# GpSimd waits for the normalised input ahead of its clears and splits, in a four-stage transformer kernel

## The reference

```
x = x + attention0(ln(x));  x = x + mixture0(ln(x))     # 12 heads of 16, relative positions; 8 experts, relu
x = x + attention1(ln(x));  x = x + mixture1(ln(x))     # the same, tanh gelu
x = x + attention2(ln(x))                               # relative positions
t = ln(x); t = t + attention3(ln(t))                    # causal
x = x + t + mixture2(ln(t))                             # capacity-limited routing, gelu
x = x + mixture3(ln(x))                                 # 8 experts and a shared one, gelu
x = x + mixture4(ln(x))                                 # 8 experts and a shared one, gated silu

ln(v)  = (v - mean(v)) / sqrt(var(v) + eps)
expert = act(v @ W1[e] + b1[e]) @ W2[e] + b2[e]         # 192 -> 768 -> 192, weighted by a top-2 gate
```

## Time and profile before

| | value |
|---|---|
| median of three runs | 514.72 us (511.82 to 517.03) |
| the profiled execution | 511.37 us, span 509.5 us, mean granted clock 0.98 |
| TensorE matmuls busy | 463.6 us, 91% of the span |
| VectorE, ScalarE, GpSimd busy | 354.0, 234.8, 171.3 us |
| chain that ended last, by engine | PE 69%, DVE 11%, issue 10%, POOL 4%, DMA 3% |
| in it by line | L951 24%, L963 10%, L975 7%, L766 6%, L1047 3%, L391 1% |
| DMA | 62.36 MB, mean 122 GB/s |

### The profile page before, as it was taken

One profiled execution on the slowest core, in us unless ns is written; L12 is line 12 of the kernel. 1 busy time (PEld: TensorE's weight loads), 2 busy tenths in 40 slices (PEclk: granted clock), 3 DMA queues, 4 the chain that ended last, 5 costly groups with the idle time before them and its releaser, 6 DMA issues.

```text
span 509.5 us, 8914 instructions
## 1 busy us (share of the span) xinstructions
PE 463.6 (91%) x3064; PEld 382.4 (75%) x3064; DVE 354.0 (69%) x780; ACT 234.8 (46%) x594; POOL 171.3 (34%) x171
## 2 busy tenths in 40 slices
PE   4989699999889799999889988899969999989997
PEld 3755499999555499999645654555759999979997
DVE  6575588998476578998476467451179899868764
ACT  1267245544156366555156337423218555627443
POOL 6026324673025415754006214310033665500000
PEclk8999999999999989999999999999989999989999
DMA  5380025650191015551169500602313555525551
GB/s 146 121 248 1 1 96 183 184 187 1 65 305 40 0 64 196 180 175 39 43 170 322 176 0 1 186 2 93 124 37 134 185 185 176 191 58 166 200 177 36
DMA packets 19347, 62.36 MB, mean 122 GB/s; under 512 B 4025, under 2 KB 6898, under 8 KB 19314
## 3 DMA queue, kind: packets, MB, share of 16 engines
q1 hardware_dynamic: 19314, 61.93, 38.0%
HBM read 59.82 MB, written 2.10 MB: 122 GB/s over the span
## 4 chain that ended last, share of the span: by engine, by line
PE 69%; DVE 11%; issue 10%; POOL 4%; DMA 3%; ACT 1%; SPq 1%; POOLq 0%; DVEq 0%
PE bank L951 24%; PE bank L963 10%; PE bank L975 7%; PE bank L766 6%; PE bank L805 3%; PE bank L977 3%; PE bank L792 3%; DVE xn L1047 3%; PE bank L661 2%; POOL rstd L391 1%; DMA rel<-rel_scratch 1%; PE bank L653 1%; PE bank L773 1%; DVE nmax L1153 1%; PE bank L674 1%
## 5 line engine op out<-in xcount | busy, mean ns | idle before, releaser
L951 PE MATMUL bank<-xT_hi,w_hi 128*128 128x256 f32 x408 | 111.7, 295 | 0.0
L600 ACT ACTIVATE hid<-bank,b 128x256 f32<-128x256 f32 x150 | 62.7, 471 | 71.0 <-PE bank L951 70.8
L1193 DVE TENSOR_TENSOR w_lo<-w,w_hi 128x512 fp32r<-128x512 f32 x102 | 93.0, 950 | 2.2 <-ACT w_hi L552 0.3
L951 PE MATMUL bank<-xT_hi,w_lo 128*128 128x256 f32 x408 | 82.6, 284 | 0.0
L443 POOL TENSOR_TENSOR w_hl<-w,consts 128x384 fp32r<-128x384 f32 x50 | 52.4, 1048 | 85.1 <-PE bank L977 85.1
L951 PEld LDWEIGHTS bank<-xT_hi,w_hi 128*128 128x128 f32 x408 | 79.2, 194 | 1.5 <-issue 1.1
L423 POOL TENSOR_TENSOR probs<-probs,rinv 128x512 f32<-128x512 f32 (+1 forms) x44 | 42.8, 991 | 101.0 <-DVE rinv L1157 100.9
L951 PEld LDWEIGHTS bank<-xT_hi,w_lo 128*128 128x128 f32 x408 | 64.3, 194 | 0.0
L975 PE MATMUL bank<-w_hl,hid_hi 128*128 128x384 f32 x200 | 61.7, 373 | 0.0
L445 POOL TENSOR_TENSOR w_hl<-w,w_hl 128x384 fp32r<-128x384 f32 x50 | 57.9, 1158 | 3.9
L963 PE MATMUL bank<-w,hid 128*128 128x192 f32 x308 | 56.5, 327 | 2.3 <-issue 2.3
(11 more groups left out here) (159 smaller groups left out, 674.3 us busy)
## 6 DMA issues: line engine op xcount, KB each, us to landing
w<-in_M_w_dram SPq DMA_DIRECT2D x34, 768.0 KB, 5.5
w<-in_M_w_dram SPq DMA_DIRECT2D x33, 576.0 KB, 3.9
w<-in_M_w_dram SPq DMA_DIRECT2D x9, 288.0 KB, 2.9
wqkv<-in_A_wqkv_dram SPq DMA_DIRECT2D x4, 432.0 KB, 7.0
rel_scratch<-relall SPq DMA_DIRECT2D x4, 372.0 KB, 2.3
wproj<-in_A_wproj_dram SPq DMA_DIRECT2D x4, 288.0 KB, 7.9
wqkv<-in_M_w_dram SPq DMA_DIRECT2D x2, 576.0 KB, 17.4
kT<-in_M_w_dram SPq DMA_DIRECT2D x2, 576.0 KB, 6.6
```

The costliest lines, as they stand in the source:

```text
L600: ins = act.activation(hid[:, 2 * b + c, :], bank[B_H[b]][:, c * T:(c + 1) * T], FUNC[cfg["act"]], bias=b1[:, kb, bass.ds(at, 1)])
L951: ins = pe.matmul(bank[B_H[b]][:, c2 * T:(c2 + 1) * T], w, xs, start=(q == 0), stop=(q == 4))
L1193: dve.tensor_tensor(w1_cols(w1_lo, b), w1_cols(w1[s], b), w1_cols(w1_hi, b).bitcast(F32), ALU.subtract)\
```

## The change

Three lines move or are added, all on GpSimd. The clear of `q_st` goes ahead of the first power. Behind that power GpSimd waits until both tiles of the first input are normalised, and only then clears the rest. And in the front of each of the five mixtures it waits, behind the power, until both tiles of that mixture's input are normalised, before it begins to split. `nln` counts the layer norms so far, two tiles each. The waits inside the loops of the experts are as before.

```diff
@@ -391,9 +391,10 @@
                 pool.tensor_tensor(rstd[:, :], var_eps[:, :], minus_half[:, :], ALU.pow).then_inc(rstd_ready, 1)
 
             pool.memset(minus_half[:, :], -0.5).then_inc(minus_half_ready, 1)
+            pool.memset(q_st[:, :, :, :], 0.0).then_inc(pool_ready, 1)
             pool.wait_ge(minus_half_ready, 1)
             ln(0)
-            pool.memset(q_st[:, :, :, :], 0.0).then_inc(pool_ready, 1)
+            pool.wait_ge(xn_ready, TT)
             pool.memset(k_st[:, :, :, :], 0.0).then_inc(pool_ready, 1)
             pool.memset(v_st[:, :, :, :], 0.0).then_inc(pool_ready, 1)
             pool.memset(kT[:, :, :, :], 0.0).then_inc(pool_ready, 1)
@@ -457,6 +458,7 @@
                 else:
                     ln(nln)
                     nln += 1
+                    pool.wait_ge(xn_ready, TT * nln)
                     if MOE[n]["split2"]:
                         for i in range(2):
                             split(n, 0, i)
```

## The result

The changed kernel takes 498.62 us (median of four runs, 496.72 to 500.07) against 513.27 (511.79 to 517.03) for the kernel before; the ratio is 0.9718, 95% interval 0.9674 to 0.9762. The forecast was 501.0 in a range of 496.5 to 507. The profiled execution took 498.38, 13.0 less than the profiled one of before; the sum had said 13.5.

The account below looks back on a forecast made before the run. TensorE's matmuls held most of the span; the removable waits were VectorE instructions held by GpSimd. 2.75 + 10.7 = 13.5 us off the profiled 511.37 gave 497.9, with 3.35 to the median 501.2, given as 501; range 496.5 to 507.

Parts of the forecast that it names:

- the sum: Whole kernel: 2.75 us at the start plus 10.7 at the mixtures, 13.5 us less.
- (a): At the start: clear of q_st ahead of the first power, 1.38 us from about 0.85 to 2.2, costs nothing.
- (b): At the start: GpSimd waits for both normalised tiles; position products at 12.05 instead of 16.48, 2.75 us after clock loss.
- an open bound: At the start: gain only 2.0 us if the clears also hold the copy of the transposed input out of PSUM.
- (c): Waits ahead of the splits of mixtures 0, 1 and 3: 8.2 us plus 2.5 from the clock, 10.7 in sum.
- The yardstick: Mixture 4, same stages without splits: 7.22 us from power to second up-matmul block, against 10.05 in mixture 0.
- The slack for the low parts: Low parts of w1 for blocks 1 and 2: each can lose one split (0.9 us), covered by 0.4 us.
- (d): Waits at mixtures 2 and 4: no split follows, so nothing gained.
- the second case: Mixture fronts: clock still falls ahead of the first up matmuls; (c) is 8.2, sum 11.0, time 503.7; chance 0.20.
- the third: At the start: VectorE not held, query bias slips between two clears; 17.2 us less, 497.5; chance 0.12.
- the fourth: Mixture fronts: moved splits hold the low parts of w1 through all four; (c) is 5.5, time 507.2; chance 0.10.
- The loops did not move: Expert loops: rival had 22 later experts each 0.9 us late, 19.8 outweighing 13.5, time 521; chance 0.03.

Follow-up runs that it names:

- the late-bias version: The changed kernel with VectorE's scaling of the query bias moved to just ahead of the queries that use it: 495.42 us, ratio 0.9647.
- The profile with the gaps: The kernel before, with GpSimd waiting for each clear to end ahead of the next; one execution, transposes of the queries at 24.86 (27.58 before).

## Why the prediction was right

**(a) right.** The clear of q_st ran from 0.78 to 2.16 and held nothing.

**(b) right in mechanism and nearly in size.** Forecast: normalised at 6.05, bias scaling up at 8.6 and held to 10.9, products at 12.05, a wait of 2 us, a low stretch costing 1.65. Measured: 5.97, 9.02 and 10.80, 11.72, 2.08, 1.67 between two profiles with and without the stretch. The transposes of the queries came 3.09 us earlier, against 2.75. That the clears do not hold VectorE's instructions that read PSUM, an open bound, is shown by the late-bias version. What the prediction did not see is that neither the hold nor the low stretch is a fixed length: the hold was 2.71 us once in five profiles with back-to-back clears, and the stretch at the start ran to about 15.5, to about 18.5 or was absent. So it is in part luck that the size came so near: in other profiles of the same start the transposes are at 22.86, 25.90 and 26.06, which would have made it 4.7, 1.7 and 1.5 us. The weights, put at 8.6, came 0.4 late, which cost nothing, since the clears bound the scaling. And the row that was to show the clock at 1.00 behind 1.30 us without a matmul covers only the idle time itself; the window behind it does show it:

```profile
129.80:133.10 3.30, 3.12 (x16) 1.00 0.02 5
```

**(c) right in mechanism and in sum; the two sizes were off.** The blocking was put at 8.2 and the clock at 2.5; the fronts gained 3.58, 3.30 and 3.57, 10.45 in sum. The kernel before with more warm-up divides it otherwise: its fronts take 8.97, 8.99 and 8.97, so 7.5 is blocking and 2.9 the clock. The yardstick, mixture 4, was at a low clock too, but lost less by it: 7.22 against 6.47 us is 0.75, where mixture 0 lost 10.05 - 8.97 = 1.08. The difference of 0.33 stood in the 2.83 that the prediction put on the blocking. That the two errors cancel in the sum is no merit of the working. The idle time of 1.1 us did keep the clock up, but that it was less than 1.30 is no rule: the front with 0.21 and 1.42 us kept it in one execution and lost it in another.
The slack for the low parts, put at 0.4 us, was 0.7.

**(d) right**: mixture 4's front stayed at 7.2, and mixture 2 needs 5.96 us from the power to the matmuls behind its router, against 5.95.

**The sum.** 3.09 + 10.45 + 0.04 = 13.58, and 12.98 arrived at the last matmuls (491.67 against 504.65). The rest is the load of the position terms: 4.60 us in attention 1 instead of 3.58, and 3.42 in attention 2 instead of 3.81. Both kernels issue it in the same order; the cause of its spread was not tried. Before, then after:

```profile
140.02 3.58 DMA rel<-rel_scratch
...
256.51 3.81 DMA rel<-rel_scratch
```

```profile
133.30 4.60 DMA rel<-rel_scratch
...
247.52 3.42 DMA rel<-rel_scratch
```

The timed gain, 14.65 us by the medians, is larger than the profiled 13.0: the fronts of before, which can have a longer low stretch than the profiled 3.4 us, are gone. The profile with the gaps, whose fronts are those of before, has 6.8 us at two of them. That the longer stretches are the cause in the runs that were only timed is argued from their mean clocks (0.960 to 0.987 for before in the groups above, 0.990 to 0.997 after), not shown instruction by instruction. The forecast of 501 lies 2.4 above the median for this reason and because it started from 514.72, where the four runs of the comparison give 513.27.

**The rivals.** The clock kept up: not the second case. VectorE was held at the start: not the third, though one profile of an unchanged start shows that the outcome can vary. The blocking was handed on, as the fourth said, but by one split for each low part and not through all four, so it cost nothing. The loops did not move: 7.21 us per expert before and after.

## What to carry to other kernels

Where VectorE normalises or scales from SBUF on the critical path, keep GpSimd's clears and splits out of that stretch with one wait, and then look for the next VectorE instruction of that kind that the moved work will hit: here one scaling, moved behind its neighbours, gave as much as the start's part had. Then cover the waits in front of matmul stages with warm-up matmuls up to the arrival of the operand: on top of the late scaling it brought 1.6 us by medians on two chips and took the spread from 4.5 us to 1.3. With VectorE still held between the tiles the same cover did not do it reliably. Judge parts of 1% in a version whose clock is quiet, since otherwise the spread is larger than the part.

## What the runs showed of the hardware

- VectorE's tensor-scalar from SBUF was held by GpSimd's back-to-back clears for 6.04 us in four profiles of five, through five instructions, and for 2.71 us in one, while with a semaphore wait between the clears it got in after 1.4. The Trainium skill (SBUF — State Buffer, section Who interferes with whom) has the lock last for one instruction; a queue without gaps was seen to keep it longer.
- A memset of VectorE (0.27 us) and its instructions that read PSUM (a copy of 0.42 us, tensor-scalars of 0.44 us each) ran beside GpSimd's clears unhindered.
- VectorE's subtraction of two SBUF operands went from 689 to 1322 ns beside GpSimd's splits.
- The granted clock stayed at the 1.2 GHz level for 13.9 us while TensorE was busy 12.8 of them, and for 10.2 us while it was busy all of them. Fronts with nearly equal waits were followed by 3.4, 6.6 and 13.9 us of low clock; the same 2.08 us of waiting at the start was followed by a low stretch in the changed kernel and by none in another profile.
- Six runs of a kernel with a mean granted clock of 1.000 in each lay within 1.3 us, 0.3%; runs of the kernel before on the same chip within 7.0.
